# One row store with two lists of blocks (41 and 30) in place of two row stores (47 and 31)

## The reference

```python
x = x + conv(_gn(x), ...)          # a filter per sample, made from the sample
t = _to_tokens(x)                  # (16, 256, 128)
t = t + attn(_ln_t(t))             # tanh(x) scores, softmax, times x
t = t + moe(_ln_t(t), ...)
# the mixture: 8 experts, hidden width 256, 2 experts for each token
scores = xf @ router_w + router_b
topk_p, topk_i = top_k(softmax(scores), 2)
gated = silu(h @ wg + bg) * (h @ wv + bv)      # h = x @ w1 + b1
out = sum over the 2 experts of topk_p * (gated @ w2 + b2)
```

## Time and profile before

| | us |
|---|---|
| median of 3 runs (388.7, 388.9, 390.78) | 388.9 |
| the profiled execution: its own time | 393.15 |
| its span, first to last instruction | 391.4 |

### The profile page before, as it was taken

The page is one execution under the profiler, slowest core; times in us unless marked ns, Lnnn a source line. Parts: engine busy times, 40 slices in busy tenths (PEclk is TensorE's granted clock), DMA queues, the critical chain, the costliest instruction groups (busy, mean ns, idle before and its releaser), DMA issues.

```text
span 391.4 us, 7583 instructions
## 1 busy us (share of the span) xinstructions
PE 329.3 (84%) x1821; PEld 257.9 (66%) x1821; DVE 235.6 (60%) x1023; ACT 150.7 (39%) x486; POOL 172.0 (44%) x195
## 2 busy tenths in 40 slices
PE   3999999999999999979786698898757999898930
PEld 2676777877777877767674486575645777675820
DVE  2424656788888787867745446566333555457924
ACT  0444334362625351403032345653223555454610
POOL 4001010204464736477365454445555555454550
PEclk9999999999999999998696989999896999899975
DMA  7725131212070000012123212222222224833306
GB/s 227 253 68 150 41 109 62 88 40 68 23 258 23 32 25 28 29 35 80 35 63 83 71 48 63 68 71 78 70 72 66 70 73 128 260 86 109 118 15 241
DMA packets 32195, 34.51 MB, mean 88 GB/s; under 512 B 5515, under 2 KB 25953, under 8 KB 31898
## 3 DMA queue, kind: packets, MB, share of 16 engines
q1 hardware_dynamic: 26624, 24.53, 20.9%
q0 software_dynamic: 4608, 8.67, 6.6%
q10 hardware_dynamic: 922, 0.84, 0.6%
HBM read 22.16 MB, written 12.75 MB: 89 GB/s over the span
## 4 chain that ended last, share of the span: by engine, by line
PE 70%; DVE 12%; issue 7%; ACT 4%; DMA 3%; another core or an unknown queue 2%; POOL 1%; DVEq 1%; SPq 0%; ACTq 0%; POOLq 0%
PE bank L1528 9%; PE bank L1508 6%; PE bank L1139 5%; PE bank L1499 5%; PE bank L1517 5%; PE bank L948 5%; PE bank L1500 4%; PE bank L1024 4%; PE bank L943 3%; PE bank L1101 3%; PE bank L1492 3%; PE bank L1064 3%; PE bank L1001 2%; PE bank L976 2%
## 5 line engine op out<-in xcount | busy, mean ns | idle before, releaser
L1281 POOL DMA_INDIRECT moe_dram<-ys,xs x78 | 76.4, 980 | 73.0 <-DVE ys L1446 47.3
L423 POOL DMA_INDIRECT rows_dram<-row,slot x64 | 63.7, 995 | 23.1 <-issue 16.1
L1446 DVE SCALAR_TENSOR_TENSOR ys<-b_all,xs,bank 128x128 f32<-128x128 f32 x78 | 27.1, 347 | 46.0 <-PE bank L1528 23.3
L1528 PE MATMUL bank<-w_all,gatedt 128*128 x312 | 51.1, 289 | 0.6 <-DVE ys L1446 0.6
L1499 PE MATMUL bank<-w_high,x_high 128*128 x78 | 39.4, 506 | 14.1 <-ACT x_high L1348 9.3
L1462 DVE SCALAR_TENSOR_TENSOR gated<-bank,xs,silu 128x256 f32<-128x256 f32 x78 | 37.5, 481 | 22.3 <-ACT silu L1359 12.2
L1359 ACT ACTIVATE silu<-bank 128x256 f32<-128x256 f32 x78 | 29.9, 384 | 41.6 <-PE bank L1508 25.8
L1528 PEld LDWEIGHTS bank<-w_all,gatedt 128*128 128x128 f32 x312 | 43.5, 202 | 1.2 <-issue 0.8
L1517 PE MATMUL bank<-const,gated 128*128 128x128 f32 x156 | 32.1, 289 | 8.6 <-issue 5.3
L1348 ACT ACTIVATE x_high<-bank 128x128 fp32r<-128x128 f32 x78 | 21.8, 281 | 42.5 <-PE bank L1492 25.4
L1508 PE MATMUL bank<-w_high,x_low 128*128 x78 | 34.7, 444 | 2.5 <-DVE x_low L1437 1.1
(11 more groups left out here) (175 smaller groups left out, 624.1 us busy)
## 6 DMA issues: line engine op xcount, KB each, us to landing
xs<-rows_dram SPq DMA_DIRECT2D x78, 66.0 KB
xc<-in_x SPq DMA_DIRECT2D x8, 256.0 KB, 2.8
wgv<-in_wg SPq DMA_DIRECT2D x8, 256.0 KB, 2.7
wgv<-in_wv SPq DMA_DIRECT2D x8, 256.0 KB, 3.0
xt<-in_xt SPq DMA_DIRECT2D x4, 512.0 KB, 4.6
xt<-moe_dram SPq DMA_DIRECT2D x8, 256.0 KB, 4.2
moe_dram<-ys,xs POOLq DMA_INDIRECT x78
const<-in_const SPq DMA_DIRECT2D x1, 1123.0 KB, 9.2
```

Source lines behind the costliest of these rows:

```text
L423: pool.indirect_dma_start(rows_dram[f >= SPLIT], bass.IndirectOffsetOnAxis(ap=slot[:, f % 2, 2 * t + k:2 * t + k + 1], axis=0), row[:, f % ...
L1281: pool.indirect_dma_start(moe_dram[half_of(j)], bass.IndirectOffsetOnAxis(ap=xs[:, u, C + 1:C + 2].bitcast(U32), axis=0), ys[:, u, :], Non ...
L1528: last = pe.matmul(bank_y[j % 2][:, 0:C], gatedt[:, j % 2, h * P:(h + 1) * P], w2_all[:, bass.ds(e * (2 * C) + h * C, C)], start=(h == 0), ...
```

## The change

`SPLIT` goes from 5 to 6, and there is one `rows_dram` and one `moe_dram`. The first list has 41 blocks: what twelve times 512 rows fill for certain, whichever experts they go to (2*6*512/128 - 7). It takes full blocks of the first six pairs alone, in the order of the experts. The second list has the other 30: first what is left of the six pairs' blocks, then the blocks that pairs 6 and 7 fill. Both lists read the same regions, so an expert's rows are rounded up once.

```diff
-SPLIT = 5
-COUNTS = tuple(2 * (end - begin) * PAIR_TOKENS // P + EXPERTS - 1 for begin, end in HALVES)
-BLOCKS = sum(COUNTS)
+SPLIT = 6
+FULL = 2 * SPLIT * PAIR_TOKENS // P - (EXPERTS - 1)
+EARLY = 2 * SPLIT * PAIR_TOKENS // P + EXPERTS - 1
+BLOCKS = 2 * TOKENS // P + EXPERTS - 1
+UPTO = (SPLIT, PAIRS)
...
 # last_pair(j) on DVE
-                    if j == 24:
-                        experts["tables"](dve, 1, 0)
-                    if j == 25:
-                        experts["tables"](dve, 1, 1)
-                    if j == 26:
-                        experts["tables"](dve, 1, 2)
+                    if j == 3:
+                        experts["second_table"](dve, 0)
+                    if 23 <= j <= 26:
+                        experts["second_table"](dve, j - 22)
...
 # rounds on DVE
                         rows_of(e)
-                        if e == LAST - 1:
-                            experts["table"](dve, 0)
...
                         exp_sum_of(e)
+                        if e == LAST - 1:
+                            experts["table"](dve, 0)
...
                     if e == SPLIT - 1:
-                        experts["tables"](dve, 0)
+                        experts["first_table"](dve)
...
 # rounds on PE
                         attention(i, d)
+                    if i == rounds - 1:
+                        experts["table_columns"](pe, 0)
...
-                    if i == rounds - 2:
-                        experts["table_columns"](pe, 0)
...
 # sync
         def rows_ready(k):
+            if k == 1:
+                write_pads()
             sp.wait_ge(S["table_ready"], k + 1)
...
-                sp.wait_ge(g["sent"][s], 16 * 2 * TILES * len(range(s, HALVES[k][1], 2)))
-
-        write_pads(0, range(E))
+                sp.wait_ge(g["sent"][s], 16 * 2 * TILES * len(range(s, UPTO[k], 2)))
...
-            e = j - (A - E)
-            if 0 <= e < E:
-                write_pads(1, (e,))
...
-            p = j - (A + U - 1)
+            p = j - (NB - SPLIT)
             if p == 0:
-                all_sent(sp, A)
+                all_sent(sp, EARLY)
...
 # sums on DVE
-            p, k = divmod(j - (NB - 2 * SPLIT - 4), 2)
+            p, k = divmod(j - max(NB - 2 * SPLIT - 4, EARLY + 4), 2)
```

More of the change, by code:

```diff
@@ L134, in build @@
     with ctx:
-        rows_dram = [nc.dram_tensor(f"rows_dram{k}", (ROWS, ROW), F32, kind="Internal").ap() for k in range(2)]
-        moe_dram = [nc.dram_tensor(f"moe_dram{k}", (2 * TOKENS, C), F32, kind="Internal").ap() for k in range(2)]
+        rows_dram = nc.dram_tensor("rows_dram", (ROWS, ROW), F32, kind="Internal").ap()
+        moe_dram = nc.dram_tensor("moe_dram", (2 * TOKENS, C), F32, kind="Internal").ap()
         const = sb("const", [P, CONST_COLS])
@@ L1374, in triangle @@
     def triangle(dve):
[L1376 to L1382 removed]
+        dve.wait_ge(S["consts"], 1)
+        dve.tensor_tensor(upto[:, :, :], spread(iota17[:, 0:2 * E], 2, 2 * E), spread(iota17[:, 0:2 * E], 1, 2 * E), ALU.is_ge).then_inc(S["triangle"], 1)
@@ L1399, in tables, with first_table @@
-        if part in (None, 1):
-            then(dve.tensor_tensor(cumt[:, :, :], upto[:, :, :], spread(nblk[:, :], 1, E), ALU.mult))
+            dve.wait_ge(S["chain"], at[0])
+        return then
+    def first_table(dve):
+        then = chain_from(dve, 0)
+        dve.wait_ge(S["consts"], 1)
+        dve.wait_ge(S["triangle"], 1)
+        dve.wait_ge(g["base_done"], SPLIT)
+        then(dve.tensor_tensor(count[:, :], base[:, SPLIT, :], region[:, 0, :], ALU.subtract))
+        then(dve.tensor_tensor(more[:, :, :], spread(count[:, :], 2, NTHR), spread(last_row[:, :], 1, E), ALU.is_gt))
+        then(dve.reduce_sum(nblk[:, 0:E], more[:, :, :], AX.X))
+        then(dve.tensor_tensor(cumt[:, 0:E, 0:E], upto[:, 0:E, 0:E], spread(nblk[:, 0:E], 1, E), ALU.mult))
+        then(dve.reduce_sum(cum[:, 0:E], cumt[:, 0:E, 0:E], AX.X))
+        dve.tensor_tensor(cum_before[:, 0:E], cum[:, 0:E], nblk[:, 0:E], ALU.subtract)
+        then(dve.tensor_scalar(past[:, 0:E], cum[:, 0:E], channel[:, 0:1], None, ALU.is_le))
+        dve.scalar_tensor_tensor(offset[:, 0:E], cum_before[:, 0:E], -float(P), region[:, 0, :], ALU.mult, ALU.add)
+        then(dve.reduce_sum(expert[:, :], past[:, 0:E], AX.X))
+        then(dve.scalar_tensor_tensor(offs[:, 0:E], iota17[:, 0:E], expert[:, 0:1], offset[:, 0:E], ALU.is_equal, ALU.mult))
+        then(dve.reduce_sum(start[:, :], offs[:, 0:E], AX.X))
+        dve.tensor_scalar(block_expert[:, :], expert[:, :], float(E - 1), None, ALU.min)
+        dve.tensor_tensor(block_row[:, :], start[:, :], channel_rows[:, :], ALU.add).then_inc(S["block_ready"], 1)
@@ new lines, in second_table @@
+    def second_table(dve, part):
[6 more added lines that the diff above has]
+        if part == 1:
+            then = chain_from(dve, 11)
+            final = base[:, PAIRS, :]
+            dve.wait_ge(g["base_done"], PAIRS)
+            dve.tensor_copy(pad_at[:, :], final[0:1, :]).then_inc(S["pad_at_ready"], 1)
+            then(dve.tensor_tensor(count[:, :], final, region[:, 0, :], ALU.subtract))
+            then(dve.tensor_tensor(more[:, :, :], spread(count[:, :], 2, NTHR), spread(threshold[:, :], 1, E), ALU.is_gt))
+            then(dve.reduce_sum(ceiling[:, :], more[:, :, :], AX.X))
+        if part == 2:
+            then = chain_from(dve, 14)
+            dve.tensor_tensor(nblk[:, 0:E], begun[:, E:], begun[:, 0:E], ALU.subtract)
+            then(dve.tensor_tensor(nblk[:, E:], ceiling[:, :], begun[:, E:], ALU.subtract))
+            then(dve.tensor_tensor(cumt[:, :, :], upto[:, :, :], spread(nblk[:, :], 1, 2 * E), ALU.mult))
@@ L1407, in tables @@
             then(dve.reduce_sum(expert[:, :], past[:, :], AX.X))
-            then(dve.scalar_tensor_tensor(offs[:, :], iota9[:, :], expert[:, 0:1], offset[:, :], ALU.is_equal, ALU.mult))
+        if part == 4:
+            then = chain_from(dve, 19)
+            dve.tensor_scalar(second[:, :], expert[:, :], float(E), -float(E), ALU.is_ge, ALU.mult)
+            then(dve.scalar_tensor_tensor(offset[:, 0:2 * E], left[:, :], float(P), region[:, :, :].rearrange("p a e -> p (a e)"),
+                                          ALU.mult, ALU.add))
+            then(dve.scalar_tensor_tensor(offs[:, :], iota17[:, :], expert[:, 0:1], offset[:, :], ALU.is_equal, ALU.mult))
+            dve.tensor_tensor(second[:, :], second[:, :], expert[:, :], ALU.add)
```

108 lines of the change are left out of this document (50 added, 58 removed).

## The result

| | before | after |
|---|---|---|
| median, us (4 runs each) | 389.84 (388.7 to 391.45) | 373.87 (373.25 to 374.77) |
| the profiled execution's own time | 393.15 | 373.25 |
| its span | 391.4 | 371.3 |

The ratio is 0.9589, 95% interval 0.9541 to 0.9638: 16.0 us less, where 9.7 were forecast. So some 2 of the first 16 us may be chance. The other 4 that the forecast lacks are not: -9.7 us would be a ratio of 0.975, above all three intervals. The profiled execution of before was 3.3 us above its median, so the two spans (20.1 apart) overstate the change.

The account below looks back on a forecast made before the run. PE, busy 84% of the span, was taken as the main bound, with holes tied to POOL's runs of indirect DMAs; -12.7 + 1.5 + 1.3 + 0.6 + 1.0 - 1.4 = -9.7 from 388.9 gave 379.2 us, range 374.5 to 384.5.

Parts of the forecast that it names:

- seven blocks: End of the block loop: seven blocks fewer at 1.82 us each, -12.7 us; bounds -10.3 and -14.8.
- first table one round later, block 0 late: Round 10 and loop start: later routing and block 0 waiting for pair 5, mostly absorbed; +1.5 us, bounds 0 and +4.
- second table: DVE in steps 3 and 23 to 26: 23 instructions instead of 14, +1.3 us; bounds 0 and +2.6.
- pads: SP's queue: first eight go, second eight move ahead of block 41's load; cost 0, with cover of only 2 us.
- sums and the first one's wait: DVE in the loop: twelve sums instead of ten, +0.6 us; first sum waits for its result load, +1.0.
- end: Behind the last block: pairs 6 and 7 remain, two sums fewer, -1.4 us; bounds -1.0 and -2.5.
- absorption: Loop start: most of block 0's delay, +2 to +3.3 us, was to vanish in the wait at 218 to 222.9.
- Together with the first table +1.5; bounds 0 and +4: Routing and loop start: combined cost of the later table and late block 0; 0 if all absorbed, +4 if nothing.
- the hole: At 218 to 222.9 us engines wait beside POOL's seven dispatches, which set its time, not the blocks.
- Blocks 40 and 41 do: Second part of the block loop: example of undisturbed blocks, each coming 1.47 us after the one before.
- Rival B: Block loop: more goes than quiet blocks, waits in proportion (-14.8 us), first sum's wait covered; 376 us, chance 0.11.
- Rival C: Second list: slow SP makes block 41 5.6 us late, then 2.9 per block; +11.3, 400 us, chance 0.04.

Follow-up runs that it names:

- a_78b: The kernel after with seven more blocks (78) and the sums moved seven steps later as well: 387.93 us, 0.9934 of the kernel before.
- b_table_late: The kernel before with the first table's work moved to round 10, so block 0 starts later; pads' addresses still copied in round 9: 391.42 us, 0.9983.
- middle column: Profile means of the two kernels of before (78 blocks) changed to start block 0 late; last block to the end 21.4 us.
- a_78: The kernel after with seven more blocks (78), which left the first sum four steps too early: 391.39 us, 1.0099 of the kernel before.

## Why the prediction was wrong, step by step

| step | forecast | measured |
|---|---|---|
| seven blocks | -12.7 | -11.4 (`a_78b`), -12.0 in profiles |
| first table one round later, block 0 late | +1.5 | -0.7 (-2.1 to +0.8) in `b_table_late`, which has the whole step; -1.7 (-3.1 to -0.3) for block 0 late alone; in profiles -2.0 to block 23 and +0.9 from there to block 41 |
| second table | +1.3 | +0.6 from block 23 to 41 (46.2 against 45.5, block 0 late in both); doubled +1.0, unclear |
| pads | 0 | 0 |
| sums and the first one's wait | +1.6 | 0 to +0.8 |
| end | -1.4 | -1.4 (-1.7 against the middle column) |

The direction was right, and so were the absorption, the pads, the end and the seven blocks within their bounds. **The step that failed is "Together with the first table +1.5; bounds 0 and +4".** Its bounds excluded a gain. The kernel with the whole step measures -0.7, 2.2 below the forecast, and the one with block 0 late alone -1.7. That is half or more of the 4.3 us that the forecast lacks against -14.0. The sums give about 1 more and the second table 0.7; the seven blocks take 0.7 to 1.3 back. What is left, 1 us or so, has no term; single profiles differ by as much in each.

What the prediction saw was half of it. It saw that a delay of block 0 vanishes in the hole beside POOL's last dispatches. It did not ask what the hole does to PE. With block 0 early, PE runs out of work there, 3.4 to 4.0 us idle, and works on block 6 with the clock partly at its lower level: 3.0 to 3.4 us from block 6 to block 7, against 1.92 and 2.06 in the two kernels of before with a late block 0. With block 0 late, the work that is still to be done fills the hole. That period gives 1.2 us of the 2.0 by which blocks 6 to 23 are shorter (34.2 and 32.1; 31.6 to 33.0 in all fifteen profiles with a late block 0, 33.5 to 34.9 in all three with an early one). The other 0.9 lies in blocks 7 to 23, where the two groups overlap (30.5 to 31.5 and 29.8 to 30.5), and stays open. The two kernels that differ from before in the late start alone are among the fifteen; so the effect belongs to the late start and not to the new lists.

A queue of scatters behind POOL's dispatches, the other explanation that suggests itself, is not in the rows. In before one scatter joined the run, at 220.07, and POOL then waited for the next result:

```profile
224.79 0.99 POOL L1281 DMA_INDIRECT moe_dram<-ys,xs  x1 [3.71 <-DVE ys L1446]
```

That the idle time is what lowers the clock is how the rows read, in eighteen profiles of eighteen; no kernel changed the one without the other. From block 23 to 41 the clock is a rival too: it was 0.86 to 0.89 in the three profiles of after and 0.92 and 0.94 in the two of before with a late block 0, so the +0.6 there is not known to be DVE's table work.

Smaller errors. The sums' +0.6 and +1.0 were priced as if nothing else stopped the engines there; the wait of 2.24 us is real, and in the total nothing of it showed. The whole forecast used a single profile of before for its periods; that the stretch from block 23 to 41 varies by 1 to 2 us from one execution to the next was not in the range. "Blocks 40 and 41 do" holds for block 41 alone: block 40 came 1.91 us after block 39. And POOL's dispatches ahead of the hole are six, not seven.

Rival B came nearest in time (376), by the wrong reason: it had the seven blocks at 14.8, and they are 11.4 to 12.0, and the wait for the first sum covered, which it was not. Rival C did not occur: SP's pads took 1.5 us each and block 41 did not wait. The range of 374.5 to 384.5 missed the first median, 373.87, by 0.6, and that is partly chance: by the later ratios after's time beside 389.84 would be 376, inside it, an estimate. The sum would have been some 4 us off all the same; the step that failed should have been allowed a gain.

## What to carry to other kernels

A delay that vanishes in an engine's idle time also takes that idle time away, and this can be worth something: ask what the engine does behind the idle time, and at what clock, and give such a step bounds on both sides of zero. Where engines stop together beside one queue's DMAs, check in the trace that a new arrangement changed the runs at all before drawing a conclusion: four arrangements here cost the same, and the one that looked best in its stretch made the next dependency 8 us later. A kernel that changes a count (78 for 71) should be looked through for everything placed relative to it, or the experiment measures a sum that stands in the wrong step, as `a_78` did.

## What the runs showed of the hardware

- Block 6 came 5.0 to 5.8 us after the start of POOL's sixth dispatch in a row in all eighteen profiles, for starts of block 0 between 202.4 and 211.3 us. With block 0 late PE was busy for 3.5 to 4.8 us of that time, so there the distance is mostly PE's own work. What the engines wait for in these holes stays open; the profile names the other waiting engines, "remote" or "issue".
- The granted TensorE clock was 0.53 to 0.61 between blocks 6 and 7 where PE had been idle for 3.4 to 4.0 us since the last dispatch (three profiles), and 1.00 where it had been idle for 0.4 to 1.5 us (fifteen).
- SP took 10.40 us for eight pads in round 9 of before, 11.96 and 12.44 us for eight beside POOL's dispatches of pair 7.
- The same two kernels compared three times gave 0.9589, 0.9641 and 0.9649, and a kernel against itself 0.9971. By these, a term below 1.5 us of 390 can't be measured by one such comparison.
